# Attention block on one core: keys and queries in three bf16 parts, values of two steps together, background work in odd steps

## The chip, the core and the metric

The kernel runs on one core of a Trainium2 chip. The metric is the device time in microseconds (us) of one execution. TensorE (PE) multiplies, ScalarE (ACT) takes the exponentials, VectorE (DVE) moves and splits results, GpSimd (POOL) adds biases, and SyncE (SP) issues every DMA.

## The reference

A pre-norm block on x of shape 2 x 2048 x 1024 (batch, position, width), float32, cut to what is computed:

```python
h = layernorm(x)
q = ((h @ Wq_d + bq_d) @ W_qk + b_qk)      # 12 latents -> 32 heads of size 4
k = h @ Wkv_d + bkv_d                      # 4 latents, shared by all 32 heads
attn = softmax(q k^T / sqrt(4))            # per batch and head, 2048 x 2048
out = (attn @ (k @ Wv_u + bv_u)) @ Wo + bo # values are formed from the same 4 latents
x = x + out
x = x + layernorm(x) @ (W^T + sum over 8 LoRA updates of rank 16) + bias
```

## The kernel before

The 4096 rows of x are cut into 8 chunks of 512 (N). The program has three stretches.

**Stage 1** makes the latents, the keys and the queries of every chunk. ACT normalises and evacuates, PE transposes and multiplies, DVE takes the statistics. DVE (`split_latents`, L1002 to L1008) splits the keys into a rounded part and a remainder. ACT and POOL (L481, L437) do it for the queries, which SP stores to DRAM (`store_q`, L310). The last chunks give a bound for the softmax shift: DVE splits that too (`split_shift`, L969 to L976) and SP stores it (`store_shifts`, L323). SP then loads the first queries (`load_q`, L330), stores the last two chunks of queries and the second batch's shifts, waits for these stores, and issues the loads of the weights that chunk 0 of attention prepares (L365, L367, L370). All this stands in SP's queue in the order written.

**Attention** runs over 8 chunks of queries. A chunk has 8 groups of 4 heads, a group has 16 key tiles of 128 keys, so a chunk has 128 steps (`STEPS`) and the kernel 1024. In a step PE makes the scores of 4 heads (`scores`, L750: four matmuls side by side, each in its own 32 rows of the array, 20 rows used); ACT takes the exponential of 128 x 2048 scores in two instructions of 1024 columns (L542); and PE multiplies the probabilities of two steps earlier (`BEHIND = 2`) with the values (`values`, L761: four heads side by side in columns of 32; a float32 matmul shows as two instructions, so 8 stand in the trace). PSUM holds three score slots (of half a step each), SBUF holds the probabilities of three steps (`PROBS = 3`). The waits that couple the two engines are these:

```python
pe.wait_ge(exp_done, 2 * (c * STEPS + step) - 1)      # scores: the first exp of the step before is done
pe.wait_ge(exp_done, 2 * (c * STEPS + step) + 2)      # values: both exps of that step are done
act.wait_ge(pv_done, c * STEPS + step - PROBS + 1)    # exp: the values of three steps earlier are done
```

At a chunk's first step `scores` waits for all exps of the chunk before, and the first two exps of a chunk wait for values 126 and 127 of the chunk before.

**Background work.** While a chunk is in attention, PE also does the projection and the feed-forward product of the chunk before it, in float32r (`dense_beside`), one small piece behind the values of a step: `project` (L784, three matmuls), `turn_xn` (L791, four transposes), `dense` (L796, three matmuls). A table sets the steps. Four tiles of 128 rows start at `TILE_AT`; within a tile `DENSE_AT = (3, 4, 6, 7, 9, 10, ...)` names 16 steps of three matmuls. Chunk 0 has the preparation of the weights in that place (`prepare`: `turn_values` L681, `turn_lora` L687, `times_wo` L699, `turn_w` L717, `lora_update` L722).

**Tail.** After the last exp, the last chunk's projection and feed-forward run alone.

## Time and profile before

| | |
|---|---|
| median of 3 runs | 2360.14 us (2355.39 to 2363.23) |
| the profiled execution, its own time | 2355.23 us |
| its span, first to last instruction | 2353.5 us |
| PE busy, share of the span | 2193.2 us, 93% |
| ACT busy | 2036.0 us, 87% |
| DVE busy | 493.6 us, 21% |
| mean granted TensorE clock | 0.978 of 2.4 GHz |
| stage 1, until the first exp | 128.8 us |
| attention chunk 0 | 254.8 us |
| attention chunks 1 to 6, each | 269.9 to 273.0 us |

"Busy" is the time in which an engine has at least one instruction under way. PE's matmuls are pipelined and their ends are modelled, so the distance from start to start tells what a group costs. A timeline row merges instructions of one line; its first number is when the first started.

### The profile page before, as it was taken

Reading aid. Unit: us, or ns where it says so; the run is one execution under the profiler, and the core shown is the slowest. Engines: PE = TensorE matmul, PEld = TensorE weight load, DVE = VectorE, ACT = ScalarE, POOL = GpSimd, SP = SyncE. Lnnn points to the kernel's source line nnn. Section 1 sums busy time; section 2 is a strip of 40 time slices with the busy share of each in tenths; the row PEclk is TensorE's granted clock in tenths of the full one; section 3 lists DMA queues with packets and bytes.
Section 4 is the critical chain, followed back from the end, with each engine's and each line's share of the span. In section 5 each row is a group of like instructions: output and inputs, shape, how many; then the busy total and the mean of one; then the engine's idle time right before and its main releaser. Section 6 shows DMA issues by size and latency. Waiting matters only on the chain. (4 is left out here: it accounts for less than half of the span.)

```text
span 2353.5 us, 35829 instructions
## 1 busy us (share of the span) xinstructions
PE 2193.2 (93%) x15021; PEld 748.3 (32%) x15021; DVE 493.6 (21%) x1265; ACT 2036.0 (87%) x2193; POOL 164.4 (7%) x83
## 2 busy tenths in 40 slices
PE   5779998999989999999989999999999999899988
PEld 3422222333323332333323332233323333233337
DVE  8521223111021110211021110211112110211115
ACT  6879998989988998999989998899989999889970
POOL 0100001000010010000010010000100000100101
PEclk9989999999999999999989999999989999999999
DMA  7342000000010001000010001000010000100010
GB/s 251 117 126 78 4 26 23 7 25 13 24 33 15 13 24 42 7 13 25 25 33 4 24 25 42 4 15 25 13 42 7 23 14 24 33 14 14 24 36 36
DMA packets 36990, 78.95 MB, mean 34 GB/s; under 512 B 13380, under 2 KB 13400, under 8 KB 36828
## 3 DMA queue, kind: packets, MB, share of 16 engines
q1 hardware_dynamic: 36828, 76.65, 9.9%
q8 instruction: 119, 1.95, 0.3%
q14 instruction: 43, 0.35, 0.0%
HBM read 54.62 MB, written 22.02 MB: 33 GB/s over the span
## 5 line engine op out<-in xcount | busy, mean ns | idle before, releaser
L542 ACT ACTIVATE probs<-ps 128x1024 f32<-128x1024 f32 x2048 | 1942.3, 1033 | 218.5 <-PE ps L750 191.8
L761 PE MATMUL ps<-probs,c_wide 128*32 128x512 f32 x8192 | 1109.2, 614 | 0.4 <-ACT probs L542 0.4
L750 PE MATMUL ps<-q_in,key_t 20*128 20x512 f32 x4096 | 521.0, 498 | 91.5 <-ACT probs L542 54.9
L796 PE MATMUL ps<-w_eff,xn_t 128*128 128x512 f32 x1536 | 477.2, 425 | 0.3 <-DVE xn_t L983 0.3
L750 PEld LDWEIGHTS ps<-q_in,key_t 20*128 20x128 f32 x4096 | 199.1, 184 | 686.2 <-ACT probs L542 466.2
L796 PEld LDWEIGHTS ps<-w_eff,xn_t 128*128 128x128 f32 x1536 | 252.9, 188 | 399.9 <-issue 353.8
L1199 DVE TENSOR_TENSOR y<-ps,y 128x512 f32<-128x512 f32 x64 | 44.2, 691 | 1141.2 <-PE ps L796 1141.2
L761 PEld LDWEIGHTS ps<-probs,c_wide 128*32 128x32 f32 x8192 | 162.3, 108 | 252.6 <-ACT probs L542 133.1
L447 POOL TENSOR_TENSOR y<-y,ffn_bias 128x1024 f32<-128x1024 f32 x32 | 76.1, 2379 | 1307.2 <-DVE xn L961 1307.2
L443 POOL TENSOR_TENSOR y<-y,attn_bias 128x1024 f32<-128x1024 f32 x32 | 75.7, 2373 | 754.6 <-DMA y<-in_L_attn_x_dram 754.5
L981 DVE CAST xn_t<-ps 128x512 fp32r<-128x512 f32 x64 | 44.2, 691 | 117.8 <-PE ps L791 117.8
L784 PE MATMUL ps<-w_vo,o_t 128*128 128x512 f32 x192 | 63.0, 443 | 1.8 <-DVE o_t L983 1.8
L1183 DVE TENSOR_TENSOR y<-ps,y 128x512 f32<-128x512 f32 x64 | 44.1, 690 | 76.2 <-PE ps L784 76.2
L791 PE MATMUL ps<-ident,xn 128*128 128x128 f32 x256 | 41.8, 290 | 11.0 <-DVE xn_t L983 8.1
L784 PEld LDWEIGHTS ps<-w_vo,o_t 128*128 128x128 f32 x192 | 33.8, 200 | 53.1 <-DVE y L1183 23.5
L1157 DVE COPY o_sb<-ps 128x512 f32<-128x512 f32 x16 | 11.1, 692 | 179.5 <-PE ps L761 179.5
L791 PEld LDWEIGHTS ps<-ident,xn 128*128 128x128 f32 x256 | 27.8, 143 | 60.8 <-DVE xn_t L983 33.5
L983 DVE TENSOR_TENSOR xn_t<-ps,xn_t 128x512 fp32r<-128x512 f32 x64 | 44.3, 692 | 11.2 <-DVEq L934 11.2
L465 ACT ACTIVATE area<-ps 128x512 f32<-128x512 f32 x64 | 38.9, 626 | 7.0 <-PE ps L566 7.0
L1186 DVE BATCH_NORM_STATS2 stats<-y 128x6 f32<-128x512 f32 x64 | 44.4, 694 | 2.2
L459 ACT ACTIVATE xn<-y,nw 128x1024 f32<-128x1024 f32 x16 | 19.8, 1254 | 12.9 <-DVE nw L992 12.9
L961 DVE TENSOR_SCALAR xn<-y,mv,nw 128x1024 f32<-128x1024 f32 x32 | 26.0, 813 | 6.1 <-DVEq L934 6.1
(121 smaller groups left out, 527.0 us busy)
## 6 DMA issues: line engine op xcount, KB each, us to landing
y<-in_L_attn_x_dram SPq DMA_DIRECT2D x48, 512.0 KB, 4.9
out_dram<-y SPq DMA_DIRECT2D x32, 512.0 KB, 4.9
q_in<-q_parts SPq DMA_DIRECT2D x256, 40.0 KB
area<-in_L_attn_x_dram SPq DMA_DIRECT2D x16, 512.0 KB, 4.4
q_parts<-q_parts_sb SPq DMA_DIRECT2D x16, 256.0 KB, 2.5
y<-in_L_attn_Wo_dram SPq DMA_DIRECT2D x1, 2048.0 KB, 9.6
xn<-in_L_attn_Wo_dram SPq DMA_DIRECT2D x1, 2048.0 KB, 14.3
y<-in_L_ffn_W_dram SPq DMA_DIRECT2D x1, 2048.0 KB, 9.2
```

Source lines behind the costliest of these rows:

```text
L443: pool.tensor_tensor(y[:, t, :], y[:, t, :], attn_bias[:, :], ALU.add).then_inc(xb_ready, 1)
L447: pool.tensor_tensor(y[:, t, :], y[:, t, :], ffn_bias[:, :], ALU.add).then_inc(yb_ready, 1)
L542: nc.scalar.activation(probs[:, step % PROBS, bass.ts(pair, 2 * N)], ps[:, 2 * (i % SCORE_SLOTS):2 * (i % SCORE_SLOTS) + 2, :] .rearrange( ...
L750: last = nc.tensor.matmul(ps[:, at, :], key_t[TILE * h:TILE * h + KEYS, bass.ts(b * KT + kt, P)], q_in[TILE * h:TILE * h + KEYS, g % 2, :] ...
L761: last = nc.tensor.matmul(ps[32 * h:32 * h + 32, SUMS, :], c_wide[:, b * KT + kt, at:at + 32], probs[:, step % PROBS, bass.ts(h, N)], star ...
L784: last = nc.tensor.matmul(ps[:, bank, :], o_t[:, a, bass.ts(t, P)], w_vo[:, b, bass.ts(n, N)], start=(i == 0), stop=(i == 2))
L791: last = nc.tensor.transpose(ps[:, bank, bass.ts(a, P)], xn[:, t, bass.ts(4 * u + a, P)], ident[:, :])
L796: last = nc.tensor.matmul(ps[:, bank, :], xn_t[:, t % 2, a, kb, :], w_eff[:, b, kb, bass.ts(half, N)], start=(kb + i == 0), stop=(kb == KB ...
L981: ch.then(nc.vector.tensor_copy(high, bank_part))
L983: nc.vector.tensor_tensor(low, bank_part, high.bitcast(F32), ALU.subtract).then_inc(moved, 1)
L1186: ch.put(nc.vector.bn_stats(stats[:, t, n, :], y[:, t, bass.ts(n, N)]))
L1199: nc.vector.tensor_tensor(y[:, t, bass.ts(half, N)], ps[:, bank, :], y[:, t, bass.ts(half, N)], ALU.add).then_inc(ffn_moved, 1)
```

## The change

Keys and queries are split into three bf16 parts instead of two float32r parts. Six products of parts are kept (`KEY_PART`, `QUERY_PART`), so a head uses 6 x 5 = 30 of its 32 rows where it used 20. The stores to DRAM are one per product, six where there were two. The split has two more operations wherever it is made. The query matmul of stage 1 reads the unfolded sums with `W_qk` held four times. In attention, values of two steps are issued together in even steps, and all background pieces stand in odd steps: the 24 x 2 matmuls of a tile go in ten bursts of five (the last of each half has four). The slot of the probabilities counts on across chunks.

```diff
-    PARTS = 2
-    ROWS = PARTS * W5
...
-    KEYS = PARTS * ROWS
-    QROW = 3 * TILE + KEYS
+    PARTS = 3
...
+    KEY_PART = (0, 0, 0, 1, 1, 2)
+    QUERY_PART = (0, 1, 2, 0, 1, 0)
+    BLOCKS = len(KEY_PART)
+    KEYS = BLOCKS * W5
+    QROW = 16
...
-        key_t = sb("key_t", [P, T], F32R)
...
-        q_in = sb("q_in", [P, 2, N], F32R)
+        key_t = sb("key_t", [P, T], BF16)
...
+        q_in = sb("q_in", [P, 2, N], BF16)
...
-        DENSE_AT = (3, 4, 6, 7, 9, 10, 12, 13, 16, 17, 19, 20, 22, 23, 25, 26)
+        DENSE_AT = (4, 6, 8, 10, 12, 18, 20, 22, 24, 26)
+        BURSTS = len(DENSE_AT) // 2
+        BURST = -(-3 * KB // BURSTS)
...
-        TILE_AT = [14, 14 + TILE_STEPS, 16 + 2 * TILE_STEPS, 17 + 3 * TILE_STEPS]
+        TILE_AT = [15, 15 + TILE_STEPS, 17 + 2 * TILE_STEPS, 17 + 3 * TILE_STEPS]
...
             def store_q(c, slot):
-                for k in range(PARTS):
-                    sp.dma_start(qd[:, k * W5:k * W5 + L, bass.ds(c * N, N)], q_parts[:, slot, k, :].bitcast(F32)).then_inc(q_stored[slot], 16)
+                for i in range(BLOCKS):
+                    sp.dma_start(qd[:, i * W5:i * W5 + L, bass.ds(c * N, N)], q_parts[:, slot, QUERY_PART[i], :]).then_inc(q_stored[slot], 16)
...
                 for j in range(CB):
-                    for k in range(PARTS):
+                    for i in range(BLOCKS):
...
-                    pool.tensor_tensor(parts[:, 1, :], q_f32[:, cols], parts[:, 0, :], ALU.subtract).then_inc(q_split, 1)
+                    pool.tensor_tensor(rest, q_f32[:, cols], parts[:, 0, :], ALU.subtract).then_inc(part_own, 1)
+                    pool.wait_ge(part_own, 1)
+                    pool.tensor_copy(parts[:, 1, :], rest).then_inc(part_own, 1)
+                    pool.wait_ge(part_own, 2)
+                    pool.tensor_tensor(parts[:, 2, :], rest, parts[:, 1, :], ALU.subtract).then_inc(part_own, 1)
...
-                        if pair == 0 and step >= PROBS:
+                        if pair == 0 and c * STEPS + step >= PROBS:
                             act.wait_ge(pv_done, c * STEPS + step - PROBS + 1)
-                        elif pair == 0 and step < STEPS % PROBS and not first:
-                            act.wait_ge(pv_done, c * STEPS + step - STEPS % PROBS + 1)
...
                         scores(c, b, step, first)
-                        if not first and step == BEHIND + 4 * KT:
-                            dense_beside(c, step)
-                        if step >= BEHIND:
-                            if (step - BEHIND) % (4 * KT) == 0 and not (first and g == 0):
-                                pe.wait_ge(o_moved, 2 * c + g // 4)
-                            values(c, b, step - BEHIND)
-                        elif not first:
-                            values(c - 1, b_before, STEPS + step - BEHIND)
+                        if step % 2 == 0:
+                            if step == 0 and not first:
+                                values(c - 1, b_before, STEPS - 2)
+                                values(c - 1, b_before, STEPS - 1)
+                            if step:
+                                if (step - BEHIND) % (4 * KT) == 0 and not (first and g == 0):
+                                    pe.wait_ge(o_moved, 2 * c + g // 4)
+                                values(c, b, step - 2)
+                                values(c, b, step - 1)
...
                 ch.then(nc.vector.tensor_copy(parts[:, 0, :], shift))
+                ch.then(nc.vector.tensor_tensor(rest, shift, parts[:, 0, :], ALU.subtract))
+                ch.then(nc.vector.tensor_copy(parts[:, 1, :], rest))
```

On PE, inside a tile's feed-forward product in attention, before: scores (`key_t`), values (`probs`), and a dense piece (`w_eff`) behind two of three steps.

```order
L750 MATMUL ps<-q_in,key_t 128x512 x4
L761 MATMUL ps<-probs,c_wide 32x512 x4
L796 MATMUL ps<-w_eff,xn_t 128x512 x3
L750 MATMUL ps<-q_in,key_t 128x512 x4
L761 MATMUL ps<-probs,c_wide 32x512 x4
L796 MATMUL ps<-w_eff,xn_t 128x512 x3
L750 MATMUL ps<-q_in,key_t 128x512 x4
L761 MATMUL ps<-probs,c_wide 32x512 x4
L750 MATMUL ps<-q_in,key_t 128x512 x4
```

The same place on PE in the changed kernel: the end of a tile's half, with its burst of four.

```order
L765 MATMUL ps<-q_in,key_t 128x512 x4
L776 MATMUL ps<-probs,c_wide 32x512 x8
L765 MATMUL ps<-q_in,key_t 128x512 x4
L821 MATMUL ps<-w_eff,xn_t 128x512 x5
L765 MATMUL ps<-q_in,key_t 128x512 x4
L776 MATMUL ps<-probs,c_wide 32x512 x8
L765 MATMUL ps<-q_in,key_t 128x512 x4
L821 MATMUL ps<-w_eff,xn_t 128x512 x4
```

Between two scores there stands now either a double group of values or a piece of background, never both.

On SP, at the seam of stage 1 and attention, before: stores of the queries (`q_parts_sb`) and of the shifts (`shift_parts`), the first load of queries, and the loads of weights.

```order
L310 DMA q_parts<-q_parts_sb 32x4x512 x6
L323 DMA q_parts<-shift_parts 32x512 x8
L330 DMA q_in<-q_parts 20x1x512 x4
L310 DMA q_parts<-q_parts_sb 32x4x512 x4
L323 DMA q_parts<-shift_parts 32x512 x8
L365 DMA area<-in_L_attn_Wv_u_dram 4x1024
L367 DMA area<-in_L_ffn_lora_B_dram 128x8x16 x8
```

And the same place in the changed kernel.

```order
L315 DMA q_parts<-q_parts_sb 32x4x512 x18
L328 DMA q_parts<-shift_parts 32x512 x24
L335 DMA q_in<-q_parts 30x512 x4
L315 DMA q_parts<-q_parts_sb 32x4x512 x12
L328 DMA q_parts<-shift_parts 32x512 x24
L370 DMA area<-in_L_attn_Wv_u_dram 4x1024
L372 DMA area<-in_L_ffn_lora_B_dram 128x8x16 x8
```

The first load of queries and the weights stand behind three times as many stores as before.

## Rows read from the trace of the kernel before

**Rows 1.** The page, busy time, share of the span, instructions, and costliest groups.

```profile
PE 2193.2 (93%) x15021; PEld 748.3 (32%) x15021; DVE 493.6 (21%) x1265; ACT 2036.0 (87%) x2193; POOL 164.4 (7%) x83
...
L542 ACT ACTIVATE probs<-ps 128x1024 f32<-128x1024 f32 x2048 | 1942.3, 1033 | 218.5 <-PE ps L750 191.8
```

**Rows 2.** Windows of chunks 0, 1, 2, 4 and 7 and of the tail.

```profile
128.79:383.54 254.75, 230.01 (x1713) 61.54 (x1713) 57.14 (x116) 238.35 (x256) 9.46 (x4) 0.97 0.17 52
...
383.54:655.44 271.90, 260.91 (x1796) 85.02 (x1796) 44.45 (x110) 243.51 (x256) 16.35 (x7) 0.98 0.07 21
655.44:925.37 269.93, 258.55 (x1796) 84.66 (x1796) 44.46 (x110) 243.33 (x256) 18.97 (x9) 0.99 0.06 21
...
1196.10:1469.06 272.96, 261.93 (x1796) 85.11 (x1796) 44.46 (x110) 243.50 (x257) 20.29 (x10) 0.98 0.06 21
...
2013.99:2281.10 267.11, 257.17 (x1788) 84.60 (x1792) 44.45 (x110) 242.34 (x256) 16.68 (x8) 0.99 0.06 19
...
2281.00:2353.50 72.50, 60.97 (x272) 47.43 (x264) 41.24 (x104) 1.06 (x2) 14.21 (x6) 0.93 0.09 36
```

**Rows 3.** Timeline, two steps with background in chunk 2.

```profile
830.62 0.96 PE L796 MATMUL ps<-w_eff,xn_t 128*128 128x512 f32 x3
...
831.51 0.50 PE L750 MATMUL ps<-q_in,key_t 20*128 20x512 f32 x4
...
831.95 1.06 PE L761 MATMUL ps<-probs,c_wide 128*32 128x512 f32 x8
...
832.05 1.94 ACT L542 ACTIVATE probs<-ps 128x1024 f32<-128x1024 f32 x2 [0.39 <-PE ps L750]
...
832.94 0.96 PE L784 MATMUL ps<-w_vo,o_t 128*128 128x512 f32 x3
...
833.83 0.50 PE L750 MATMUL ps<-q_in,key_t 20*128 20x512 f32 x4
```

**Rows 4.** Timeline, steps without background in chunk 1.

```profile
410.36 1.07 PE L761 MATMUL ps<-probs,c_wide 128*32 128x512 f32 x8
...
411.76 0.51 PE L750 MATMUL ps<-q_in,key_t 20*128 20x512 f32 x4 [0.33 <-ACT probs L542]
...
413.59 0.51 PE L750 MATMUL ps<-q_in,key_t 20*128 20x512 f32 x4 [0.33 <-ACT probs L542]
```

**Rows 5.** Timeline of attention's last steps; two narrower windows of it; the chain's dense part.

```profile
2276.46 5.61 ACT L542 ACTIVATE probs<-ps 128x1024 f32<-128x1024 f32 x6 [0.38 <-PE ps L750]
...
2277.53 0.50 PE L750 MATMUL ps<-q_in,key_t 20*128 20x512 f32 x4
...
2279.80 1.92 PE L761 MATMUL ps<-probs,c_wide 128*32 128x512 f32 x16
...
2280.25 1.47 PE L761 MATMUL ps<-probs,c_wide 128*32 128x512 f32 x12
...
2280.68 1.04 PE L761 MATMUL ps<-probs,c_wide 128*32 128x512 f32 x8
...
2338.32 11.23 PE ps L796 x48
```

**Rows 6.** Weight loads by form, 700 to 900 us: busy us, mean ns.

```profile
L750 PEld LDWEIGHTS ps<-q_in,key_t 20*128 20x128 f32 x380 | 18.2, 181 | 51.8 <-ACT probs L542 28.9 <-issue 22.9
...
L761 PEld LDWEIGHTS ps<-probs,c_wide 128*32 128x32 f32 x760 | 15.0, 108 | 22.9 <-ACT probs L542 15.1 <-issue 7.8
```

**Rows 7.** Timeline of the seam between chunks 1 and 2.

```profile
650.97 0.51 PE L750 MATMUL ps<-q_in,key_t 20*128 20x512 f32 x4 [0.34 <-ACT probs L542]
...
653.81 0.51 PE L750 MATMUL ps<-q_in,key_t 20*128 20x512 f32 x4 [1.34 <-ACT probs L542]
...
655.44 1.94 ACT L542 ACTIVATE probs<-ps 128x1024 f32<-128x1024 f32 x2 [1.78 <-PE ps L761]
```

**Rows 8.** Windows: around that seam, and unthrottled steps without background.

```profile
652.50:660.50 8.00, 4.28 (x36) 1.07 (x36) 0.69 (x1) 5.45 (x7) 4.72 (x2) 1.00 0.27 88
...
660.50:663.90 3.40, 3.07 (x19) 0.94 (x16) 0.00 (x0) 3.25 (x4) 0.00 (x0) 0.66 0.00 0
...
409.00:419.00 10.00, 8.72 (x76) 2.58 (x68) 2.83 (x5) 9.60 (x11) 2.38 (x1) 1.00 0.03 6
```

**Rows 9.** Timeline of SP at the seam of stage 1 and attention.

```profile
117.35 3.97 SPq L323 DMA_DIRECT2D q_parts<-shift_parts  x8
121.44 2.73 SPq L330 DMA_DIRECT2D q_in<-q_parts  x4
124.22 2.79 SPq L310 DMA_DIRECT2D q_parts<-q_parts_sb  x4
127.05 5.20 SPq L323 DMA_DIRECT2D q_parts<-shift_parts  x8
134.73 0.31 SPq L365 DMA_DIRECT2D area<-in_L_attn_Wv_u_dram  x1
135.10 4.94 SPq L367 DMA_DIRECT2D area<-in_L_ffn_lora_B_dram  x8
```

**Rows 10.** Timeline of the same place, other engines.

```profile
116.63 0.69 DVE L976 TENSOR_TENSOR shift_parts<-shift_f,shift_parts 128x512 fp32r<-128x512 f32 x1 [0.18 <-DVEq L934]
...
127.95 0.80 PE L750 MATMUL ps<-q_in,key_t 20*128 20x512 f32 x4 [3.15 <-DMA q_in<-q_parts]
...
143.73 0.20 PE L682 MATMUL ps<-ident,small 8*128 8x8 f32 x1
...
150.77 1.11 PE L687 MATMUL ps<-ident,area 128*128 128x128 f32 x4 [3.83 <-DVE bv_wide L1119]
```

**Rows 11.** Timeline at 1.2 GHz in chunk 0.

```profile
154.41 0.80 PE L750 MATMUL ps<-q_in,key_t 20*128 20x512 f32 x4
...
155.14 1.67 PE L761 MATMUL ps<-probs,c_wide 128*32 128x512 f32 x8
...
155.25 1.94 ACT L542 ACTIVATE probs<-ps 128x1024 f32<-128x1024 f32 x2 [0.66 <-PE ps L750]
```

**Rows 12.** Timeline, one chunk of stage 1; page, landing of the stores.

```profile
69.54 1.27 POOL L437 TENSOR_TENSOR q_parts_sb<-area,q_parts_sb 128x512 f32<-128x512 f32 x1 [11.16 <-POOLq L436]
...
75.00 0.16 DVE L992 SCALAR_TENSOR_TENSOR nw<-mv,nw 128x4 f32<-128x4 f32 x1 [0.17 <-DVEq L934]
...
81.80 1.28 ACT L459 ACTIVATE xn<-y,nw 128x1024 f32<-128x1024 f32 x1
...
q_parts<-q_parts_sb SPq DMA_DIRECT2D x16, 256.0 KB, 2.5
```

More of the change, by code:

```diff
@@ L556, in _ @@
             pe.wait_ge(down_ok, 1)
-            nc.tensor.matmul(ps[:, 7, 0:1], bias_row, ones[0:1, 0:1], start=True, stop=True).then_inc(bias_ps, 1)
+            nc.tensor.matmul(ps[:, 7, 0:1], bias_row, ones[0:1, 0:1], start=True, stop=True)
+            nc.tensor.matmul(ps[:, 7, 1:2], wqk_sb[0:32, :], bqk_sb[0:32, 2:3], start=True, stop=True).then_inc(bias_ps, 1)
             pe.wait_ge(down_ok, 3)
@@ L592, in use_latents @@
                 pe.wait_ge(q_read, START + c)
-                nc.tensor.matmul(ps[:, 7, :], wqk_sb[96:P, :], lat[96:P, slot, :], start=True, stop=True
-                                 ).then_inc(q_ps, 1)
+                nc.tensor.matmul(ps[:, 7, :], wqk_sb[:, :], down_part[:, :], start=True, stop=True).then_inc(q_ps, 1)
             def largest(b):
@@ L761, in values @@
                     last = nc.tensor.matmul(ps[32 * h:32 * h + 32, SUMS, :], c_wide[:, b * KT + kt, at:at + 32],
-                                            probs[:, step % PROBS, bass.ts(h, N)], start=(kt == 0 and g % 4 == 0),
+                                            probs[:, (c * STEPS + step) % PROBS, bass.ts(h, N)], start=(kt == 0 and g % 4 == 0),
                                             stop=(kt == KT - 1 and g % 4 == 3))
@@ L799, in dense, with dense_burst @@
                     last.then_inc(ffn_ready, 1)
+            PRODUCTS = [(kb, i) for kb in range(KB) for i in range(3)]
+            def dense_burst(p, t, half, j):
+                for kb, i in PRODUCTS[BURST * j:BURST * (j + 1)]:
+                    a, b = THREE[i]
+                    last = nc.tensor.matmul(ps[:, SHARED, :], xn_t[:, t % 2, a, kb, :], w_eff[:, b, kb, bass.ts(half, N)],
+                                            start=(kb + i == 0), stop=(kb == KB - 1 and i == 2))
+                if j == BURSTS - 1:
+                    last.then_inc(ffn_ready, 1)
             def dense_beside(c, step):
@@ L966, in split_shift @@
                 ch = Chain(v_shift)
-                shift = shift_f[0:rows, 0, :]
+                shift, rest = shift_f[0:rows, 0, :], shift_f[0:rows, 1, :]
                 parts = shift_parts[0:rows]
@@ L974, in split_shift @@
                 ch.then(nc.vector.tensor_copy(parts[:, 0, :], shift))
+                ch.then(nc.vector.tensor_tensor(rest, shift, parts[:, 0, :], ALU.subtract))
+                ch.then(nc.vector.tensor_copy(parts[:, 1, :], rest))
                 ch.end()
-                nc.vector.tensor_tensor(parts[:, 1, :], shift, parts[:, 0, :].bitcast(F32), ALU.subtract).then_inc(done, 1)
+                nc.vector.tensor_tensor(parts[:, 2, :], rest, parts[:, 1, :], ALU.subtract).then_inc(done, 1)
             def split_three_pass(high, low, bank_part, moved):
@@ L1001, in split_latents @@
                 dve.wait_ge(lat_ready, START + c + 1)
-                ch.put(nc.vector.tensor_copy(part_b[:, :], src))
+                rest = part_f[:, 0, :]
+                ch.put(nc.vector.tensor_copy(part_b[:, 0, :], src))
                 ch.put(nc.vector.tensor_reduce(c_max[:, bass.ds(c, 1)], src, AX.X, ALU.max, apply_absolute_value=True))
                 ch.wait()
-                ch.end()
                 if meanwhile:
                     meanwhile()
-                nc.vector.scalar_tensor_tensor(out=key_t[:, cols], in0=part_b[:, :].bitcast(F32), scalar=less_high[:, 0:1], in1=src,
+                ch.then(nc.vector.scalar_tensor_tensor(out=rest, in0=part_b[:, 0, :], scalar=less_high[:, 0:1], in1=src,
+                                                       op0=ALU.mult, op1=ALU.add))
+                ch.then(nc.vector.tensor_copy(part_b[:, 1, :], rest))
+                ch.end()
+                nc.vector.scalar_tensor_tensor(out=key_t[:, cols], in0=part_b[:, 1, :], scalar=less_high[:, 1:2], in1=rest,
                                                op0=ALU.mult, op1=ALU.add).then_inc(lat_split, 1)
@@ L1200, in add_dense @@
                                         ).then_inc(ffn_moved, 1)
-            for k in range(3):
+            for k in range(4):
                 move_w(k)
             move_o(0, 0, True)
-            move_w(3)
             norm_o(0, 0)
```

114 lines of the change are left out of this document (61 added, 53 removed).

## The prediction

> **What bounds the kernel now.** I read the page first, then the chunks one by one, then single steps. The page shows PE busy for 93% and ACT for 87% of the span, and ACT idle for 218.5 us before its exps, released by PE's scores for 191.8 of them [rows 1]. So the two hand the bound to and fro. The windows show where: attention is 128.8 to 2281 us, its chunks are alike (269.9 to 273.0 us), and the last, which has no seam behind it, takes 267.1 [rows 2]. The rest, stage 1 and a tail of 72.5 us, is 201 us. Inside a chunk there are two kinds of steps. One with background is paced by PE: from scores to scores 831.51 to 833.83, 2.32 us [rows 3]. One without is paced by ACT: 411.76 to 413.59, 1.83 us [rows 4], two exps of 0.91. 72 steps of a chunk carry three float32r matmuls. Both engines have slack in the other's steps, and only PSUM's three score slots lie between them, so little of it is averaged out.
>
> **Prices of the pieces on PE, start to start, at 2.4 GHz.** Scores 0.43 (831.51 to 831.95). Values of one step 1.00 (831.95 to 832.94). Three background matmuls 0.89 (832.94 to 833.83) [rows 3]. Background matmuls in a run cost 11.23/48 = 0.23 each, so a burst of five costs 0.89 + 2 x 0.23 = 1.36 and one of four 1.13. Two steps of values in a row stand in the kernel's last steps: 2279.80, 2280.25, 2280.68, spaced 0.45 and 0.43 [rows 5]. The second step of values adds two such passes, so the double group costs 1.00 + 2 x 0.43 = 1.86 instead of 2.00. Across the engines: from the start of scores to the exp 0.54 [rows 3], and from the start of a step's first exp to the next scores 1.07 (2276.46 to 2277.53) [rows 5].
>
> **The new order costs by itself.** Let E be the start of the first exp of an odd step. The even step's scores start at E + 1.07, cost 0.43, and then the double group holds PE for 1.86. The odd step's scores start at E + 3.36, and the first exp of the next odd step at E + 3.90, where ACT alone would be ready at 2 x 1.83 = 3.66. So a pair with little background, a light pair, takes 3.90 and no longer 3.66: the work of two steps in one lump comes between two scores. A heavy pair, with five background matmuls, is bound by PE alone: 0.43 + 1.86 + 0.43 + 1.36 = 4.08. Two steps with background took 4.64, but were two thirds of the tile's steps. A burst of four makes 3.85 and hides under the light pair's 3.90. Projections (0.89) and transposes hide there too: there is room for 0.54 + 1.07 - 0.43 = 1.18. A chunk has 4 tiles x 2 halves x 4 = 32 heavy and 32 light pairs.
>
> **What bf16 does to the scores.** The trace has no bf16 matmul. The array's work is 512 columns as before, in 30 rows instead of 20, side by side as before, so I cost the extra rows at nothing. What can shrink is the loading of the 128 key columns, which nothing covers, since it starts with the group. Loads of 128 columns take 181 ns and loads of 32 take 108 [rows 6]: 73 ns for 96 columns, 0.10 us for 128. So a group of scores gets shorter by 0 (nothing changes) to 0.10 (the load vanishes). Nearest for a narrow load is the 32-column one of the values: the spacings of 0.45 and 0.43 say that it exposes only 0.02 [rows 5]. I take this for two-byte keys: 0.08 saved, scores 0.35, scores to exp 0.46. That is a choice, and the largest one here. It enters each pair twice: light 3.90 - 0.16 = 3.74, heavy 4.08 - 0.16 = 3.92.
>
> The Trainium skill, "TensorE: Matmul & The Clock Gate", section on weight-path perf modes, says that weights are loaded fast when there are 128 of them and the type is not FP32. By its figures the load falls to between a half and a quarter, which as an estimate is 0.05 to 0.08 us and a sum some 20 us higher to the same as mine. No run here shows it yet; the float32r load at full length is no contradiction if float32r counts as FP32.
>
> **Chunks 1 to 7.** 32 x 3.74 + 32 x 3.92 = 245.1. The seam now costs about 4.6 (average of chunks 1 to 6, 271.7, less 267.1 [rows 2]). There scores wait for the last exp (650.97 to 653.81) and the exp waits 1.63 instead of 0.54 for values [rows 7], and for 3.4 us behind it the clock is lower [rows 8]. The wait for all exps stays (about 0.9); the exp's wait goes, for values 125 are long done. I put 3 us on it, between 0.9 and 4.6. So 248.1 in place of 271.7, six times: -141.8; and 245.1 in place of 267.1 once: -22.0.
>
> **The seam of stage 1 and attention.** SP issues DMAs one by one, and the new stores stand ahead of what attention needs. `split_shift` has two more DVE operations (0.69 and 0.43, with waits about 1.6): from 117.3 to 119.0 [rows 10]. Then 24 shift stores at 0.50 to 0.65 each [rows 9]; with 0.55, 13.2: 132.2. Loading queries takes 2.73, and PE starts 3.8 after the last issue, as now (124.17 to 127.95): 138.8 in place of 127.95. Step 1's exp waits for all stores of queries, whose buffer the probabilities take over: 12 at 0.70, and 2.5 to land [rows 9, 12]: 146. Behind them 24 shift stores at 0.65: 159. Now 2.5 us pass to the first weight, then 5.3 for nine issues [rows 9], some 2 to land: 168.8. `turn_values` at step 7 waits for these; now it runs at 143.7 [rows 10], and without the queue it would come at about 158. From there 121 steps are left: 60.5 pairs of 3.74, 226.3 (I take the pieces of the preparation to hide in the odd steps, as the projections do); `turn_lora` still waits for DVE, 7.04 behind `turn_values` (143.73 to 150.77) [rows 10] where two steps give 3.74: 3.3; seam and a low clock after the two stalls: 3. Chunk 1 starts at 401.4 instead of 383.5: +17.9.
>
> **Costed at nothing.** Stage 1 itself: POOL's two more operations (1.27 each) and four more stores delay the next tiles by about 5 us, and DVE does two more operations in `split_latents`; the statistics are ready at 75.0 and wanted at 81.8 [rows 12], a cover of 6.8. Gone, it would cost up to 1.5 a chunk, 9 us. The first loads have three small DMAs more, under DVE's statistics. The tail is the same code.
>
> **The sum.** -141.8 - 22.0 + 17.9 = -146 on the span of 2353.5: 2207.6. The execution is 1.7 us longer than its span, and its 2355.2 lies 5 below the median. On the median: 2214, taken as **2215**.
>
> **Rivals.**
> (1) Scores in bf16 cost what they cost in float32r. Pairs are 3.90 and 4.08, a chunk 255.4 + 3: -80.0 in six, -11.7 in the last, and chunk 0 ends at 410.9, +27.4. The gain is 64: **2296**. For it: 512 columns take 0.23 in a run, more than half of the group's 0.43, and stay. Against it: the load that nothing covers. At the other end (0.10 saved, 0.04 less in each of 512 pairs) it would be 2195.
> (2) TensorE's clock falls in light pairs. Before it fell at the seam, PE had been busy for 4.28 of 8.00 us; in steps without background, where it held, for 8.72 of 10.00 [rows 8]. In a light pair PE would be busy for about 2.75 of 3.74, less than in such steps now. At 1.2 GHz scores to values is 0.73 and scores to exp 0.84 [rows 11], so with the double group doubled a light pair takes 1.07 + 0.73 + 3.72 + 0.84 = 6.36, 2.6 more. With 10 to 40 of the 284 light pairs: +26 to +104, about **2280**.
> (3) Slower than before. It is the same mechanism past its point: the gain of 146 is used up at 146/2.6 = 56 light pairs, eight in each chunk, so if the clock stayed low in each chunk's first 15 steps, which have least background, it would be about even, and with half of the light pairs (142) it is **2580**.
> (4) No change: scores as dear as in (1), and 25 light pairs at the low clock, **2360**.
>
> **How the numbers follow.** The forecast, cheap loads and the clock kept, 0.57, by itself 2185 to 2245; (1) 0.28; (2) 0.10; (3) 0.03; (4) 0.02. The range 2185 to 2302 takes in the forecast, most of (1) with its 2296, and half of (2). About 0.3%, 7 us, is what a measurement of this kernel can tell from no change: faster 0.95, same 0.02, slower 0.03.
>
> **What the profile would show.** Light pairs of 3.74 and heavy ones of 3.92 from scores to scores, two apart; distance from scores to the double group 0.35, or 0.43 for (1); the weight loads of the scores near 110 ns instead of 181. ACT's idle time before exps in every odd step, from 218.5 to some 100 to 150 us in all. Chunks of 248 us. The first exp at about 139.6, and PE waiting at step 7 until about 169. The clock above 0.97. The forecast fails if double groups leave a gap between their two steps, if scores stay at 0.43, or if the clock column shows halves in light pairs.

## The result and the profile after

The changed kernel takes **2167.64 us** (median of 4, 2166.49 to 2171.91), the kernel before 2358.77 us (4 runs, 2355.39 to 2363.23): a ratio of 0.9192 with an interval of 0.9172 to 0.9212, 8.1% faster. The forecast was 2215 us, in a range of 2185 to 2302. The direction was right, but the time lies 17 us below the range: the gain is 191 us and not 144. One execution of each kernel was profiled; that of the changed kernel was its longest (2171.91 us).

The page of the changed kernel: busy time, the granted clock in tenths, and the costliest groups (busy us, mean ns, idle us before and who ended it).

```profile
PE 1954.2 (90%) x15023; PEld 717.3 (33%) x15023; DVE 511.2 (24%) x1292; ACT 2005.0 (92%) x2193; POOL 180.3 (8%) x100
...
PEclk9978999999999999999999999999999999999999
...
L554 ACT ACTIVATE probs<-ps 128x1024 f32<-128x1024 f32 x2048 | 1911.5, 1029 | 64.7 <-PE ps L765 37.9
...
L765 PEld LDWEIGHTS ps<-q_in,key_t 30*128 30x128 bf16 x4096 | 103.8, 91 | 766.5 <-ACT probs L554 712.0
```

The line of ACT is the result in short: its exps take nearly what they took (1029 ns each against 1033), but its idle time before them went from 218.5 us [rows 1] to 64.7; 100 to 150 were forecast. A weight load of the scores is recorded with 91 ns, where it was 181 [rows 6] and 110 were forecast.

The windows of chunks 0, 1, 2 and 7 and of the tail (from first exp to first exp; columns as in [rows 2]):

```profile
138.36:396.47 258.11, 207.30 (x1709) 55.55 (x1713) 55.70 (x117) 237.38 (x257) 9.48 (x4) 0.95 0.18 56
396.47:641.14 244.67, 230.33 (x1800) 81.10 (x1804) 44.50 (x110) 239.15 (x256) 14.27 (x6) 0.99 0.05 15
641.14:884.17 243.03, 228.70 (x1800) 80.92 (x1804) 44.50 (x110) 239.15 (x256) 18.99 (x8) 1.00 0.07 22
...
1856.29:2097.80 241.51, 228.15 (x1792) 80.70 (x1792) 43.81 (x109) 238.21 (x256) 19.01 (x8) 1.00 0.07 22
2097.80:2170.10 72.30, 61.17 (x273) 47.56 (x272) 41.95 (x105) 0.94 (x2) 14.24 (x6) 0.93 0.14 51
```

Chunks 2 to 6 take 243.0 us each (269.9 to 273.0 before), 248.1 was forecast. The last window has 241.5 where the forecast put 245.1, but it ends at the start of the last exp and so lacks one exp; to that exp's end the last chunk takes 242.5. The granted clock is 1.00 in chunks 2 to 7: nothing of the clock rival came there. Chunk 0 takes 258.1, the tail is as it was.

The timeline of a light pair (723.50 to 727.19) and a heavy pair (729.37 to 733.24) in chunk 2, matmuls only (start, us, count, idle before):

```profile
723.50 0.39 PE L765 MATMUL ps<-q_in,key_t 30*128 30x512 bf16 x4 [0.53 <-ACT probs L554]
...
727.19 0.39 PE L765 MATMUL ps<-q_in,key_t 30*128 30x512 bf16 x4 [0.53 <-ACT probs L554]
...
729.37 0.39 PE L765 MATMUL ps<-q_in,key_t 30*128 30x512 bf16 x4
...
729.70 1.43 PE L821 MATMUL ps<-w_eff,xn_t 128*128 128x512 f32 x5
...
731.06 0.39 PE L765 MATMUL ps<-q_in,key_t 30*128 30x512 bf16 x4
...
731.38 1.93 PE L776 MATMUL ps<-probs,c_wide 128*32 128x512 f32 x16
...
733.24 0.39 PE L765 MATMUL ps<-q_in,key_t 30*128 30x512 bf16 x4
```

From start to start: scores 0.33 (729.37 to 729.70), burst of five 1.36, scores 0.32, double group 1.86, scores again. The heavy pair takes 3.87 us, 1.69 of it in the step with the burst and 2.18 in the step with the values. The light pair takes 3.69. The group of scores cost 0.43 before [rows 3]. Over all groups between 450 and 2000 us the median is 0.430 us before and 0.325 now.

The seam between chunks 2 and 3:

```profile
881.23 0.39 PE L765 MATMUL ps<-q_in,key_t 30*128 30x512 bf16 x4
...
883.75 0.40 PE L765 MATMUL ps<-q_in,key_t 30*128 30x512 bf16 x4 [0.99 <-ACT probs L554]
...
884.07 1.92 PE L776 MATMUL ps<-probs,c_wide 128*32 128x512 f32 x16
884.17 1.94 ACT L554 ACTIVATE probs<-ps 128x1024 f32<-128x1024 f32 x2 [0.57 <-PE ps L765]
...
885.93 0.39 PE L765 MATMUL ps<-q_in,key_t 30*128 30x512 bf16 x4
```

The first exp comes 0.42 after its scores, where [rows 7] show 1.63, and the two steps around the seam take 4.70, about 1.0 more than a light pair. 32 pairs of 3.69 and 32 of 3.87 make 241.9 us, and a full chunk takes 1.1 more. From the second seam on the granted clock stays at 1.00; before, it was 0.66 behind the seam of [rows 8].

SP at the start of attention (columns: start of the first issue, time of all issues, how many):

```profile
121.04 12.45 SPq L328 DMA_DIRECT2D q_parts<-shift_parts  x24
133.62 2.72 SPq L335 DMA_DIRECT2D q_in<-q_parts  x4
136.39 7.64 SPq L315 DMA_DIRECT2D q_parts<-q_parts_sb  x12
144.07 11.27 SPq L328 DMA_DIRECT2D q_parts<-shift_parts  x24
...
158.37 5.55 SPq L372 DMA_DIRECT2D area<-in_L_ffn_lora_B_dram  x8
```

The same place on ACT and PE:

```profile
137.71 0.61 PE L765 MATMUL ps<-q_in,key_t 30*128 30x512 bf16 x4 [7.10 <-DMA q_in<-q_parts]
...
145.66 3.77 ACT L554 ACTIVATE probs<-ps 128x1024 f32<-128x1024 f32 x4 [5.36 <-DMA q_parts<-q_parts_sb]
...
166.64 0.90 PE L693 MATMUL ps<-ident,area 4*128 4x4 f32 x7 [8.13 <-DMA area<-in_L_ffn_lora_B_dram]
```

The queue did what was worked out for it: first scores at 137.7 (138.8 forecast), step 1's exp at 145.7 (146), `turn_values` at 166.6 (168.8) after 8.1 us of PE waiting for the weights. The order of the waits is as forecast, but that the times agree so closely is luck. The first batch of shift stores began 2 us later than forecast, while its issues cost 0.52 instead of 0.55, and those of the second batch 0.47 instead of 0.65. And this execution came late out of stage 1, because DVE's statistics waited for a load of x:

```profile
72.00 5.01 DVE L964 BATCH_NORM_STATS2 stats<-y 128x6 f32<-128x512 f32 x8 [3.00 <-DMA y<-in_L_attn_x_dram]
```

The same wait is 0.31 us in the kernel with counting slots (below), whose stage 1 is the same. In the seven kernels of the next section with this stage 1 and this order in SP's queue, `turn_values` came at 161.5 to 164.9 us, 4 to 7 before the forecast.

### The profile page after: what moved, and what is told of

It is laid out like the page before. It is cut to its first block and busy times, and to the rows that moved or that the text cites. A ratio compares the mean times of both kernels' runs of the same rounds, so it can differ in the third digit from the quotient of the medians.

```text
span 2170.1 us, 35966 instructions
## 1 busy us (share of the span) xinstructions
PE 1954.2 (90%) x15023; PEld 717.3 (33%) x15023; DVE 511.2 (24%) x1292; ACT 2005.0 (92%) x2193; POOL 180.3 (8%) x100
## 3 DMA queue, kind: packets, MB, share of 16 engines
q1 hardware_dynamic: 48954, 76.69, 10.6%
## 5 line engine op out<-in xcount | busy, mean ns | idle before, releaser
L554 ACT ACTIVATE probs<-ps 128x1024 f32<-128x1024 f32 x2048 | 1911.5, 1029 | 64.7 <-PE ps L765 37.9
L776 PE MATMUL ps<-probs,c_wide 128*32 128x512 f32 x8192 | 990.6, 601 | 0.0
L765 PE MATMUL ps<-q_in,key_t 30*128 30x512 bf16 x4096 | 405.2, 385 | 146.4 <-ACT probs L554 137.1
L821 PE MATMUL ps<-w_eff,xn_t 128*128 128x512 f32 x1344 | 387.0, 416 | 0.0
L765 PEld LDWEIGHTS ps<-q_in,key_t 30*128 30x128 bf16 x4096 | 103.8, 91 | 766.5 <-ACT probs L554 712.0
L776 PEld LDWEIGHTS ps<-probs,c_wide 128*32 128x32 f32 x8192 | 213.3, 109 | 427.3 <-issue 241.3
L821 PEld LDWEIGHTS ps<-w_eff,xn_t 128*128 128x128 f32 x1344 | 230.4, 188 | 98.5 <-issue 63.5
L811 PE MATMUL ps<-w_eff,xn_t 128*128 128x512 f32 x192 | 45.4, 393 | 0.3 <-DVE xn_t L1011 0.3
L811 PEld LDWEIGHTS ps<-w_eff,xn_t 128*128 128x128 f32 x192 | 35.6, 188 | 8.8 <-DVE xn_t L1011 1.6
```

Of the source, the lines that this page charges most:

```text
L554: nc.scalar.activation(probs[:, (c * STEPS + step) % PROBS, bass.ts(pair, 2 * N)], ps[:, 2 * (i % SCORE_SLOTS):2 * (i % SCORE_SLOTS) + 2, ...
L765: last = nc.tensor.matmul(ps[:, at, :], key_t[TILE * h:TILE * h + KEYS, bass.ts(b * KT + kt, P)], q_in[TILE * h:TILE * h + KEYS, g % 2, :] ...
L776: last = nc.tensor.matmul(ps[32 * h:32 * h + 32, SUMS, :], c_wide[:, b * KT + kt, at:at + 32], probs[:, (c * STEPS + step) % PROBS, bass.t ...
L811: last = nc.tensor.matmul(ps[:, bank, :], xn_t[:, t % 2, a, kb, :], w_eff[:, b, kb, bass.ts(half, N)], start=(kb + i == 0), stop=(kb == KB ...
L821: last = nc.tensor.matmul(ps[:, SHARED, :], xn_t[:, t % 2, a, kb, :], w_eff[:, b, kb, bass.ts(half, N)], start=(kb + i == 0), stop=(kb == ...
```

## The experiments

All of them ran beside the kernel before, whose median in each group of runs was 2358.4 to 2359.7 us.

**The two halves of the change.** First the new order alone: two float32r parts as before.

```diff
-    PARTS = 3
+    PARTS = 2
...
-        key_t = sb("key_t", [P, T], BF16)
+        key_t = sb("key_t", [P, T], F32R)
...
-        q_in = sb("q_in", [P, 2, N], BF16)
+        q_in = sb("q_in", [P, 2, N], F32R)
```

> The kernel before (two float32r parts, 20 rows, two stores per chunk) with the new order alone: values of two steps together, background in odd steps in bursts of five, the probabilities' slot counting on. By the prices of the prediction with scores at 0.43 us a light pair takes 3.90 and a heavy one 4.08, a chunk 255.4 plus about 1.6 at its seam; chunk 0 comes out as now, since its stalls are the same. Theory A (order and types each give what the price list says): 6 x (271.7 - 257.0) + 11.7 = 100 off, about 2258 us, ratio to before 0.957. Rival B (the types are what counts, the order alone is paid back by the lump of two steps): 2330 us or more. Rival C (light pairs lose the clock in this order when scores are float32r): above 2280 with halves in the clock column.

Measured: 2255.86 us (2253.65 to 2259.7), ratio 0.9569 [0.9553, 0.9585]; chunks of 256.7, the last one 255.0. The forecast for the pairs without cheaper scores was 3.90 and 4.08. A heavy pair of this kernel:

```profile
704.30 0.51 PE L753 MATMUL ps<-q_in,key_t 20*128 20x512 f32 x4 [0.32 <-ACT probs L542]
704.73 1.92 PE L764 MATMUL ps<-probs,c_wide 128*32 128x512 f32 x16
706.59 0.51 PE L753 MATMUL ps<-q_in,key_t 20*128 20x512 f32 x4
707.02 1.42 PE L809 MATMUL ps<-w_eff,xn_t 128*128 128x512 f32 x5
708.38 0.51 PE L753 MATMUL ps<-q_in,key_t 20*128 20x512 f32 x4
```

704.30 to 708.38 is 4.08 to the last digit, and its pieces 0.43 + 1.86 + 0.43 + 1.36 are those of the prediction. So the new order is worth 103 us by itself.

Then the types alone: three bf16 parts, values of one step in every step, and the background where it was.

```diff
-        DENSE_AT = (4, 6, 8, 10, 12, 18, 20, 22, 24, 26)
...
+        DENSE_AT = (3, 4, 6, 7, 9, 10, 12, 13, 16, 17, 19, 20, 22, 23, 25, 26)
```

> The changed kernel with the old order: three bf16 parts, 30 rows, six stores per chunk, but values of one step in every step, dense pieces of three in 16 steps of a tile, and the old waits at the seam. Theory A (scores shorter by 0.11 us, nothing else): a step with background takes 2.21 instead of 2.32, a step without is paced by ACT as before; of 72 steps with background about 0.11 each plus what the neighbours gain, so 8 to 12 us less a chunk, 260 to 264; chunk 0 longer by 20 for the stores, less 5. About 2295 us (2280 to 2315), ratio 0.973. Rival B (the types carry the whole gain): below 2230.

Measured: 2280.28 us (2279.36 to 2280.45), ratio 0.9666 [0.965, 0.9682], at the lower edge of what A gave: 78.7 us. A step with background takes 2.22 instead of 2.32 in the trace. The halves add up to 181.8, and together they bring 191.1. So neither depends much on the other. The granted clock is still at its lower level (1.2 GHz) for 3.4 to 10 us behind seams here: this kernel has the old seam.

**The scores' rows.** With four products instead of six the scores use 20 rows of the array instead of 30, and a third of the shift stores falls away.

```diff
-    KEY_PART = (0, 0, 0, 1, 1, 2)
-    QUERY_PART = (0, 1, 2, 0, 1, 0)
+    KEY_PART = (0, 0, 1, 2)
+    QUERY_PART = (0, 1, 0, 0)
```

> The changed kernel with four products of parts instead of six (key parts 0, 0, 1, 2 with query parts 0, 1, 0, 0; the products of first key part with third query part and of the two second parts are left out). A head uses 20 rows as in the kernel before, and there are four stores for each six. Theory A (scores are shorter because of the narrow keys' load, whatever the rows): scores to values stays 0.32 to 0.33, chunks stay 243.0; only the seam of stage 1 gets shorter, 8 shift stores (4.2 us) and 4 query stores (2.6) before exp step 1, then 8 shift stores (3.8), so the weights come 10 earlier: 2158. Rival B (30 rows cost streaming time): scores shorter, chunks 238 to 241, total 2125 to 2145.

Measured: 2157.55 us (2155.08 to 2159.87), ratio 0.9147 [0.9128, 0.9165]. Chunks 2 to 6 take 243.04 as in the changed kernel and a load still 91 ns: the ten more rows cost nothing. The gain of 10 us comes from the start, where chunk 0 takes 248.9 instead of 258.1 with fewer stores in SP's queue.

**The feed-forward in bf16.** The same cheap load for the burst's 128x128 weights: both parts of the normalised rows and of the weights are bf16.

```diff
-        w_eff = nc.alloc_sbuf_tensor_at("w_eff", [P, 2, KB, D], F32R, offset=area_at)
+        w_eff = nc.alloc_sbuf_tensor_at("w_eff", [P, 2, KB, D], BF16, offset=area_at)
...
-        xn_t = sb("xn_t", [P, 2, 2, KB, P], F32R)
+        xn_t = nc.alloc_sbuf_tensor_at("xn_t", [P, 2, 2, KB, P], BF16, offset=xn_t_at)
```

> The changed kernel with the feed-forward product in two bf16 parts instead of two float32r parts (three products as before; its parts carry fewer bits). Theory A (what bf16 takes away is the load of 128 columns that the first matmul behind a change of tiling exposes, 0.10 us, and 0.02 of each matmul's spacing of 0.235): a burst of five takes 1.18 instead of 1.36, the odd step of a heavy pair falls to 0.33 + 1.18 = 1.51, which is the length of the loop scores, exp, next scores (1.50), so heavy pairs become light ones, 3.69. A chunk is 32 x 0.17 = 5.5 shorter: 237.5; the tail 3 shorter: 2126. Rival B (only row-tiled scores gain from bf16, full-array matmuls do not): 2168.

Measured: 2130.47 us (2129.08 to 2131.22), ratio 0.9031 [0.9014, 0.9047]; chunks of 237.93. A burst and the pair behind it:

```profile
724.71 1.25 PE L822 MATMUL ps<-w_eff,xn_t 128*128 128x512 bf16 x5
725.90 0.40 PE L766 MATMUL ps<-q_in,key_t 30*128 30x512 bf16 x4
726.23 1.92 PE L777 MATMUL ps<-probs,c_wide 128*32 128x512 f32 x16
728.08 0.39 PE L766 MATMUL ps<-q_in,key_t 30*128 30x512 bf16 x4
...
729.59 0.39 PE L766 MATMUL ps<-q_in,key_t 30*128 30x512 bf16 x4
```

The pair with its burst is now 3.69 (725.90 to 729.59), like one without. The burst of five from 724.71 to the scores at 725.90 takes 1.19 where float32r took 1.36. The step with the burst takes 1.51 (728.08 to 729.59): PE's work in it, 0.33 + 1.19, is now level with the way from scores through the exp to the next scores (1.50, below).

**What the double group is worth.** Types, background and seam of the changed kernel, but one step's values in every step.

```diff
-                        if step % 2 == 0:
...
-                                values(c, b, step - 2)
-                                values(c, b, step - 1)
+                        if step >= BEHIND:
...
+                            values(c, b, step - BEHIND)
```

> The changed kernel with values of one step in every step again, all else as in it: bursts of five stay in odd steps. On PE a heavy pair is then 2 x (0.32 + 1.00) + 1.36 = 4.00 instead of 3.86; a light pair has no lump and falls to ACT's pace, 3.66 instead of 3.69. Chunk 32 x 4.00 + 32 x 3.66 = 245.1 against 241.9: 3.2 more, seven times, and chunk 0 about 2 less. Theory A: 2188 us, 20 more than the changed kernel. Rival B (the pairing of the values is the main gain): 2230 or more. Rival C (the lump costs more than its switch saves): equal or faster, 2165.

Measured: 2247.9 us (2247.03 to 2248.57), ratio 0.9529 [0.9513, 0.9545]. This missed A by 60 us and fell on B's side. Pairing the values is worth 80 us, not 20. The timeline of a heavy pair:

```profile
1318.21 0.39 PE L765 MATMUL ps<-q_in,key_t 30*128 30x512 bf16 x4
...
1318.53 1.06 PE L776 MATMUL ps<-probs,c_wide 128*32 128x512 f32 x8
1318.64 3.77 ACT L554 ACTIVATE probs<-ps 128x1024 f32<-128x1024 f32 x4 [0.41 <-PE ps L765]
...
1319.72 0.40 PE L765 MATMUL ps<-q_in,key_t 30*128 30x512 bf16 x4
...
1322.39 0.39 PE L765 MATMUL ps<-q_in,key_t 30*128 30x512 bf16 x4
```

What I had not seen: scores can be only one step ahead, so from scores to scores a step takes the longer of two things. One is PE's work between them. The other is the loop over ACT: scores to exp 0.43, exp to next scores 1.07, together 1.50. In this kernel the step without a burst has work for 0.33 + 1.00 = 1.33 and waits for the loop (1318.21 to 1319.72, 1.51). The step with the burst has 0.33 + 1.00 + 1.36 = 2.69 (1319.72 to 1322.39, 2.67). The pair is 4.18. In a heavy pair of the changed kernel the two works are 2.18 and 1.69, both above 1.50, and PE waits for nothing. Of the 0.32 between the pairs, 0.14 are the fewer passes of the double group and 0.17 the idle time that the even spread avoids. Chunk 0 has no such bursts and takes the same in both kernels (258.3 and 258.1 us). In the other seven, 32 heavy pairs of 0.32 make 72 us, and the eight pairs with a burst of four, each 0.3 longer, another 17. The other pairs and the seam give a few back: the chunks are 11.5 longer each, 80.6 in all, and 80 were measured.

That rule came after the run, so it got a forecast of its own: the same edit on the kernel with the feed-forward in bf16.

```diff
-                        if step % 2 == 0:
+                        if step >= BEHIND:
...
-        w_eff = nc.alloc_sbuf_tensor_at("w_eff", [P, 2, KB, D], F32R, offset=area_at)
+        w_eff = nc.alloc_sbuf_tensor_at("w_eff", [P, 2, KB, D], BF16, offset=area_at)
```

> Values of one step in every step, as in the kernel with values apart, and the feed-forward product in bf16 parts, which takes 0.17 off every burst of five. It asks why a heavy pair took 4.18 there and not PE's 4.00. Theory A (the loop: after a long step PE cannot catch up, since the next scores need an exp that only starts when this step's scores are done, 0.43 + 1.07 = 1.50 from scores to scores; a pair is the longer step plus the larger of 1.50 and PE's work in the other): 0.33 + 1.00 + 1.18 + 1.50 = 4.01, a chunk 254.5 - 32 x 0.17 = 249, total 2204. Rival B (PE's work alone sets it, the 0.18 was something else): also 0.17 off by this change alone, so the total cannot tell, but the trace can: the even step from scores to scores is 1.50 with PE idle before it under A, and PE has no gap under B. Rival C (the burst is hidden once it is short, ACT's pace 3.64): chunk 235 to 240.

Measured: 2200.0 us (2199.23 to 2202.77), ratio 0.9325 [0.9311, 0.934]. Its steps are 1.51 (1321.23 to 1322.74) and 2.51 (to 1325.25). The rule gives 1.50 and 0.33 + 1.00 + 1.19 = 2.52. By the trace the weight loads of the scores at 1322.74 waited for an exp, as theory A has it, and those at 1325.25 did not.

**The seam.** Back: the buffer of the probabilities starts again in each chunk, with the old waits.

```diff
-                        if pair == 0 and c * STEPS + step >= PROBS:
+                        if pair == 0 and step >= PROBS:
                             act.wait_ge(pv_done, c * STEPS + step - PROBS + 1)
-                        nc.scalar.activation(probs[:, (c * STEPS + step) % PROBS, bass.ts(pair, 2 * N)],
+                        elif pair == 0 and step < STEPS % PROBS and not first:
+                            act.wait_ge(pv_done, c * STEPS + step - STEPS % PROBS + 1)
+                        nc.scalar.activation(probs[:, step % PROBS, bass.ts(pair, 2 * N)],
```

> The changed kernel with the probabilities' slot starting anew in each chunk, so that the first two exps of a chunk wait for values 126 and 127 of the chunk before, as in the kernel before. Values 126 are done about 1.3 us after the seam's scores, values 127 about 2.2 after them, against exps that now start 0.43 and 2.2 after them. Theory A (the seam's gain is this wait alone): 1 to 1.5 us a chunk, 7 to 10 in all, 2177. Rival B (the wait also leaves PE idle enough that the clock falls at each seam, as in the kernel before): 3 to 4.5 a chunk, 2190 to 2200, with a low clock behind every seam.

Measured: 2179.1 us (2176.37 to 2180.02), ratio 0.9235 [0.9219, 0.925], 11.5 more than the changed kernel. The windows ahead of the low clock and in it at one seam (clock third from the end):

```profile
883.69:886.30 2.61, 1.12 (x12) 0.10 (x4) 0.69 (x1) 2.61 (x3) 0.00 (x0) 1.00 0.85 272
...
887.20:890.60 3.40, 3.40 (x20) 0.54 (x12) 0.00 (x0) 2.09 (x3) 2.36 (x1) 0.51 0.66 192
```

With the old waits PE is busy for 1.12 of 2.61 us at the seam, and then the granted clock is at its lower level for 3.4 us. So it is behind five of the six seams from the second on. In the changed kernel the clock stays at 1.00 over the same six. The chunks of this kernel are 243.8 to 245.5. So theory A has the size (2177) and rival B's low clock came too, at less than the price that B put on it.

The other way: the score slots count on across chunks too, so that the first scores of a chunk no longer wait for the last exp.

```diff
-                if step:
+                if c * STEPS + step:
                     pe.wait_ge(exp_done, 2 * (c * STEPS + step) - 1)
-                elif not first:
-                    pe.wait_ge(exp_done, 2 * c * STEPS)
...
-                    at = 2 * ((2 * step + h // 2) % SCORE_SLOTS) + h % 2
+                    at = 2 * ((2 * (c * STEPS + step) + h // 2) % SCORE_SLOTS) + h % 2
```

> The changed kernel with the three score slots counting on across chunks, so that a chunk's first scores wait for one exp less. Theory A: the two steps at a seam take 3.69 like a light pair instead of 2.51 + 2.19 = 4.70, 1.0 less, seven times: 2161. Rival B (something else holds the seam, the last dense burst or DVE): 2168.

Measured: 2161.03 us (2160.52 to 2161.81), ratio 0.9163 [0.9147, 0.918]; chunks of 242.11, 0.9 less.

**SP's queue.** The stores of the first chunk's shifts go first, then the load of queries; the rest of the first batch follows, then the weights, and only then the second batch.

```diff
-            store_shifts(0)
+            store_shifts(0, (0,))
...
+            store_shifts(0, range(1, CB))
+            sp.wait_ge(t_ready, START + CHUNKS * KB)
+            sp.dma_start(wv_in, wv_u).then_inc(lora_in, 16)
...
             store_shifts(1)
```

> The changed kernel with another order in SP's queue at the seam of stage 1: only the six shift stores of the first chunk stand ahead of the first load of queries, then the query stores, the other shifts of batch 0, the weights that step 7 wants, and only then the shifts of batch 1; DVE's wait for the shift stores moves behind the preparation. Theory A (chunk 0's two stalls are SP's issue time): first scores 9.4 earlier, exp step 1 9.4 earlier, weights 14 earlier: turn_values at about 152.7 instead of 166.6, total 2154. Rival B (step 7's stall only moves to the weights of step 17 or to the second load of queries): 2160 to 2168.

Measured: 2161.79 us (2160.13 to 2165.68), ratio 0.9163 [0.9147, 0.918]: B. `turn_values` ran at 150.45 instead of 166.64, but further on PE stood again:

```profile
177.85 0.61 PE L766 MATMUL ps<-q_in,key_t 30*128 30x512 bf16 x4 [6.92 <-DMA q_in<-q_parts]
```

and SP shows why:

```profile
163.47 0.41 SPq L376 DMA_DIRECT2D y<-in_L_attn_Wo_dram  x1
...
164.81 7.86 SPq L335 DMA_DIRECT2D q_in<-q_parts  x8
```

The second load of queries, issued at 164.81, came behind the two 2 MB loads of `Wo` (the first is shown). The stall that was taken away at step 7 had hidden that one. Chunk 0 took 255.3 instead of 258.1.

**Less work for PE.** Probabilities and values in plain bf16, in one pass instead of float32's two.

```diff
-        c_wide = sb("c_wide", [P, T // P, CW + 32], F32)
+        c_wide = sb("c_wide", [P, T // P, CW + 32], BF16)
...
-        probs = sb("probs", [P, PROBS, 4 * N], F32)
+        probs = nc.alloc_sbuf_tensor_at("probs", [P, PROBS, 4 * N], BF16, offset=probs_at)
```

> The changed kernel with probabilities and values in plain bf16, one part each, so that a step of values is one pass of 512 columns and not two double ones (the probabilities lose their low bits). It asks what bounds attention once PE has room. Theory A (ACT's exps are the floor, 1.81 to 1.83 a step): every pair 3.64 to 3.66, a chunk 233 to 234.5, total 2168 - 8 x 9.3 = 2092. Rival B (the switches of tiling and the loop still cost): pairs of 3.7, 2120. Rival C (writing two bytes makes ACT's exps faster): below 2080.

Measured: 2161.16 us (2156.87 to 2163.79), ratio 0.9161 [0.9146, 0.9175], a miss by 69 us. Half of PE's largest work is gone, and almost nothing came of it. The windows of chunks 1 and 2:

```profile
396.00:640.00 244.00, 186.21 (x1300) 74.16 (x1300) 44.45 (x110) 238.56 (x260) 14.15 (x6) 0.84 0.05 16
640.00:884.00 244.00, 184.34 (x1308) 73.65 (x1306) 45.15 (x111) 239.64 (x261) 19.42 (x9) 0.86 0.08 27
```

and a burst of five at either clock:

```profile
1155.31 0.61 PE L766 MATMUL ps<-q_in,key_t 30*128 30x512 bf16 x4 [0.25 <-ACT probs L555]
...
1155.85 2.50 PE L822 MATMUL ps<-w_eff,xn_t 128*128 128x512 f32 x5
...
1158.29 0.61 PE L766 MATMUL ps<-q_in,key_t 30*128 30x512 bf16 x4
...
1164.00 1.42 PE L822 MATMUL ps<-w_eff,xn_t 128*128 128x512 f32 x5
```

PE is busy for 184 to 186 of 244 us instead of 229 of 243, and the granted clock is 0.84 to 0.86 where it was 1.00. Most steps hide the low clock under ACT's 1.83. A burst that falls into it does not: 1155.31 to 1158.29 is 2.98. Six chunks average 240.7 where 128 x 1.83 is 234.2, and chunk 0 took 266.3. By the records of chunks 1 to 6, the 33 steps whose burst fell wholly into the low clock took 2.94 each, 36 us more than 33 steps of 1.83. That is nearly all of the 39 us by which the six chunks exceed ACT's pace. This is the mechanism of the prediction's rival (2), on another kernel and in its bursts.

**All that paid.** The feed-forward in bf16, the slots counting on, and SP's order, this time with the second load of queries ahead of `Wo`.

```diff
+            load_q(0, 1, 1, q_loaded[1])
             for half in range(2):
                 sp.dma_start(w_stage[half][:, :, :].rearrange("p t (a n) -> p (t a) n", n=N),
```

> The changed kernel with the three things that gave time put together: feed-forward product in bf16 parts, score slots counting on across chunks, and the other order in SP's queue, now with the second load of queries ahead of the two loads of Wo. Theory A (they add up): 2130.5 - 6.6 (seams) - 5.9 (queue) - 7 (the 7 us that PE waited for the second load of queries) = 2111. Rival B (the queue's gain is lost again to a later wait, Wo at step 17): 2118 to 2125.

Measured: **2110.39 us** (2108.96 to 2111.83), ratio 0.894 [0.8928, 0.8952]: 10.6% below the kernel before, and by the two ratios (0.8940 / 0.9192) 2.7% below the changed one. Chunks take 237.0, chunk 0 246.1, and the wait for the second load of queries is gone.

## Why the prediction was right, and where it was not

**The mechanism was right, and its largest term was too small.** The time fell out of the range because of how much a group of scores gained, "0.08 saved, scores 0.35". The order makes PE's pairs, priced piece by piece: with dear scores 3.90 and 4.08 were forecast and measured, and the kernel with the order alone came 2 us from its expectation. The extra rows cost nothing, as put. SP's queue held to within 2.2 us at each of the three places named, though partly by luck, as said above. Rivals (1), (3) and (4) are out by the trace: scores to values is 0.33, not 0.43, and the clock is 1.00 in chunks 2 to 7.

**The sizes were off, all on one side.** The forecast span was 2207.6 and the measured one is 2170.1, 37.5 less:

- The scores, -22. The term "0.08 saved" is the step that failed: the group went from 0.430 to 0.325, 0.105 less, past even the end of the bounds called "the load vanishes". Pairs are 3.69 and 3.87 instead of 3.74 and 3.92, and 64 of them 241.9 instead of 245.1; 7 x 3.2 = 22. What went is told below.
- The seam, -10. "I put 3 us on it" measured 1.4 on average of chunks 1 to 6 (1459.8 - 6 x 241.9 = 8.4). The 3 held a share for a low clock that is gone from all seams but the first; the kernel with the old waits has it, and costs 11.5 us more in all.
- Chunk 0, -5: it ended at 396.5 instead of 401.4, with 2.2 us from earlier weights and the rest from the pairs. In the kernel with counting slots, whose chunk 0 has the same code, it ended at 392.1: the issues of the stores were priced too dear, and a late end of stage 1 hid part of that.

The last window ends at the start of the last exp, and that makes the rest, 0.4. The same window end stands in the prediction: 267.1 us lacks one exp (0.96 us), so the seam before cost about 3.7 and not 4.6, and the whole 245.1 was set against a chunk that lacked an exp.

The other 10 us are no part of the kernel. The profiled execution of before lay 5 below its median, and I added that to the span; 2214 was rounded up; and the profiled execution of the changed kernel lay 4.3 above its median. Which execution is profiled is chance.

**The range** ended at 2185, and both low bounds were in the text: scores at 0.33 give 2195, a seam at 0.9 another -12.6. Taken together they make 2182. It was not on them that I set the low end, and nothing was left in it for the 10 us of the median and for chunk 0.

**What bf16 took from the scores.** The prediction took all of it for the weight load and held the 512 columns fixed. The bursts of the feed-forward show both parts, matmul by matmul. The second and third matmul of the burst that starts at 729.70 in the changed kernel (float32r), and of the one that starts at 724.71 in the kernel with the feed-forward in bf16, each from its own narrow window:

```profile
730.03 0.40 PE L821 MATMUL ps<-w_eff,xn_t 128*128 128x512 f32 x1
...
730.27 0.40 PE L821 MATMUL ps<-w_eff,xn_t 128*128 128x512 f32 x1
```

```profile
724.94 0.38 PE L822 MATMUL ps<-w_eff,xn_t 128*128 128x512 bf16 x1
...
725.16 0.38 PE L822 MATMUL ps<-w_eff,xn_t 128*128 128x512 bf16 x1
```

Over all bursts of five with complete records the median spacing is 0.335 us behind the first matmul and 0.234 behind the next ones in float32r, 0.226 and 0.216 in bf16. So a first load exposes 0.10 in float32r and 0.01 in bf16, and every matmul of 512 columns is 0.02 shorter besides. Together that is 0.11, about what a group of scores gained. For the scores themselves, where the four matmuls start at once, this split is argued from the bursts and not shown.

**A step that was right for too small a reason.** The double group was put into the sum for its passes, 0.14 a pair. In the pair's sum its larger effect was there without being named: it fills the step that has no burst up to the loop's 1.50 and beyond. Only the run with values apart, where I expected 20 us and saw 80, showed it; the rule it led to then gave the next kernel to within 4 us.

**The Trainium skill**, "TensorE: Matmul & The Clock Gate", section on weight-path perf modes, lets a bf16 load take half the time of a float32 one. The records agree, 91 ns against 181. The spacing does not follow the record in proportion: of the 0.10 that the first load of a burst exposed, nine tenths went and not half. The quarter in the prediction's estimate is what the section gives as theory for fp8. And with half of the 0.10 saved, a pair would have been 0.06 longer in each of 512, as an estimate a sum some 30 us higher and not 20. That the page's rule treats float32r as float32 is supported by the feed-forward, where the same loads of 128 columns take 188 ns in float32r and 98 in bf16.

**Open.** The first exp came at 133.9 us in the kernel with counting slots and at 138.4 in the changed one, which have the same stage 1. By the trace 3.4 of these 4.4 us were lost in stage 1, most of them behind the load of x that DVE waited for (3.00 us against 0.31). Why that load landed late in one execution I did not find out. It moves the gains of the queue and of the twenty rows, read from single profiled executions, by a few us.

## What to carry to other kernels

Where two engines hand work to and fro with one step of lookahead, write down for each step the work of the first engine and the loop over the second. The step costs the larger, so a lump is cheap if it fills a step that would have waited, and dear on top of a full one. A weight load that stands first in a group can be paid in part (0.10 of its 0.19 us here, in float32r): look at the spacing of groups, not at the load's record, and try the two-byte type. Give TensorE less work only where its granted clock stays up, and when a transfer is moved ahead in a queue, look for the next one behind it that the old stall was hiding.
